# Spreading a chunk's score, value, state and output groups differently over its four steps

## What is computed

```python
# attention layer: 16 heads of size 64 for Q and K, 16 for V, 12 levels
Q, K, V = x @ Wq.T, x @ Wk.T, x @ Wv.T
dt  = softplus(x @ Wdt.T + dt_bias);  cg = cumsum(-exp(A_log) * dt, axis=1)
Lam = softplus(Lp * (x @ Wdl.T))
W[t,s] = (Q[t] . K[s]) / 8 * exp(cg[t] - cg[s]) * Lam[t, level(t, s)]   # s <= t
o = (W @ V) @ Wout.T + x;  x = layernorm(x + layernorm(o) * ln_g + ln_b)
# recurrent layer over the 2 entries, 256 features
c = sigmoid(x wf + c uf + bf) * c + sigmoid(x wi + c ui + bi) * tanh(x wc + c uc + bc)
x = layernorm(x + tanh(x wo + c_final uo + bo))
```

## Time and profile before

| | us |
|---|---|
| three runs | 703.26, 699.67, 698.87 |
| median | 699.67 |
| the profiled execution's own time | 703.26 |
| its span, first to last instruction | 701.5 |

### The profile page before, as it was taken

How to read it: one execution, slowest core, us unless ns; L and a number is a source line. 1 busy time by engine, 2 the same in 40 slices (tenths; PEclk the granted TensorE clock), 3 DMA queues, 4 the chain that set the end, 5 groups by cost and what they waited for, 6 DMA issues and landing times.

```text
span 701.5 us, 22072 instructions
## 1 busy us (share of the span) xinstructions
PE 670.3 (96%) x9172; PEld 603.3 (86%) x9172; DVE 475.2 (68%) x1067; ACT 339.6 (48%) x759; POOL 355.5 (51%) x476
## 2 busy tenths in 40 slices
PE   5889999999999999999999999999997999999994
PEld 3779999998999999899999999999986788888894
DVE  2843768688776968675877769686877445454546
ACT  4545455544444453555444444545443434555555
POOL 1652755645564646466565636565464224344434
PEclk9989999999999999999999999999999899999997
DMA  8020312203050402112150503121222000000002
GB/s 296 26 57 18 80 40 58 68 31 96 3 95 7 92 21 78 35 33 64 35 95 3 95 9 90 35 63 49 35 66 93 1 1 0 31 32 31 30 31 91
DMA packets 53588, 37.09 MB, mean 53 GB/s; under 512 B 5360, under 2 KB 52080, under 8 KB 53488
## 3 DMA queue, kind: packets, MB, share of 16 engines
q1 hardware_dynamic: 53488, 35.67, 20.2%
HBM read 30.41 MB, written 5.24 MB: 51 GB/s over the span
## 4 chain that ended last, share of the span: by engine, by line
PE 88%; DVE 3%; DMA 2%; POOL 2%; ACT 2%; SPq 1%; issue 1%; DVEq 0%; ACTq 0%
PE bank L378 64%; PE bank L381 6%; PE bank L467 5%; PE bank L400 5%; PE bank L432 4%; PE bank L496 4%; SPq L325 1%; DMA xt<-in_wffn 1%; DMA bv<-in_bcv 1%; DVE t L966 1%; ACT t L735 1%; POOL wL L1333 1%; POOL t L1333 0%; DVE ng L963 0%; DVE t L963 0%
## 5 line engine op out<-in xcount | busy, mean ns | idle before, releaser
L378 PE MATMUL bank<-xH,wH 128*128 128x256 f32 x480 | 148.3, 309 | 2.4 <-ACT KT L735 1.1
L378 PE MATMUL bank<-xL,wH 128*128 128x256 f32 x480 | 136.1, 284 | 0.0
L378 PE MATMUL bank<-xH,wL 128*128 128x256 f32 x480 | 135.5, 282 | 0.0
L735 ACT ACTIVATE QT<-bank 128x512 f32<-128x512 f32 x64 | 38.2, 597 | 144.1 <-PE bank L378 144.1
L963 DVE TENSOR_TENSOR W<-bank,E 128x512 f32<-128x512 f32 x128 | 82.2, 684 | 35.6 <-PE bank L378 35.6
L378 PEld LDWEIGHTS bank<-xH,wH 128*128 128x128 f32 x480 | 91.4, 190 | 10.2 <-issue 9.0
L378 PEld LDWEIGHTS bank<-xL,wH 128*128 128x128 f32 x480 | 91.7, 191 | 0.4
L378 PEld LDWEIGHTS bank<-xH,wL 128*128 128x128 f32 x480 | 91.7, 191 | 0.0
L735 ACT ACTIVATE E<-bank 128x512 f32<-128x512 f32 x128 | 66.1, 603 | 17.4 <-PE bank L400 17.4
L378 PE MATMUL bank<-QT,KT 64*128 64x128 f32 x1024 | 65.9, 279 | 0.6 <-ACT E L735 0.6
L735 ACT ACTIVATE KT<-bank 128x512 f32<-128x512 f32 x64 | 38.0, 594 | 54.1 <-PE bank L378 54.0
(11 more groups left out here) (149 smaller groups left out, 1660.5 us busy)
## 6 DMA issues: line engine op xcount, KB each, us to landing
cB<-scr SPq DMA_DIRECT2D x240, 64.0 KB, 3.0
xt<-in_xT SPq DMA_DIRECT2D x16, 256.0 KB, 3.7
xs<-in_x SPq DMA_DIRECT2D x16, 256.0 KB, 4.1
out<-xs SPq DMA_DIRECT2D x16, 256.0 KB, 2.1
xt<-in_wffn SPq DMA_DIRECT2D x8, 256.0 KB, 3.2
QT<-in_wqk SPq DMA_DIRECT2D x4, 256.0 KB, 5.8
KT<-in_wqk SPq DMA_DIRECT2D x4, 256.0 KB, 6.9
scr<-cT SPq DMA_DIRECT2D x16, 64.0 KB, 1.9
```

The costliest lines, as they stand in the source:

```text
L378: return e.matmul(o, a, b, start=start, stop=stop)
L735: return e.activation(o, i, f, **kw)
```

## The change

It touches no instruction's operands, only the order on PE, ACT and DVE, and with it the order in which the two shared banks are handed out (`misc_jobs`). On PE, weigh(ci-1, 1) goes from n = 0 to n = 1, behind inter; scores(ci, 1) goes from n = 1 to n = 2; state goes from n = 3 to n = 2, behind scores(ci, 1); out_proj(ci-1) goes from n = 2 to n = 3; turn_coefs goes in front of the projection of its step. ACT takes turn_coefs in front of the projection's copy. DVE takes turn_y and out_proj one step later and state one step earlier.

```diff
--- before.py
+++ after.py
@@ -76,7 +76,7 @@
             out += [("keys", ci, 0), ("keys", ci, 1)]
         if s % 4 == 1 and cc:
             out += [("inter", ci, 0), ("inter", ci, 1)]
-        if s % 4 == 3 and cc < CB - 1:
+        if s % 4 == 2 and cc < CB - 1:
             out += [("state", ci, 0)]
     for sg, j in token_jobs(s):
         if j == 3:
@@ -690,27 +690,28 @@
                     exponents(ci)
                 if (c1 := chunk_at(s, 4)) is not None:
                     weigh(c1, 0)
-                    weigh(c1, 1)
                 if 0 <= ci < NC:
                     if n == 0:
                         keys(ci)
                     if n == 1:
                         scores(ci, 0)
-                        scores(ci, 1)
                         if ci in INTER:
                             inter(ci)
-                    if n == 3 and ci in STATE:
-                        state(ci)
-                if (c1 := chunk_at(s, 6)) is not None:
+                    if n == 2:
+                        scores(ci, 1)
+                        if ci in STATE:
+                            state(ci)
+                if (c1 := chunk_at(s, 5)) is not None:
+                    weigh(c1, 1)
+                if (c1 := chunk_at(s, 7)) is not None:
                     out_proj(c1)
                 for sg, j in token_jobs(s):
                     if j == 3:
                         decays(sg)
+                    if j == 5:
+                        turn_coefs(sg)
                 for sg, j in project_jobs(s):
                     project(sg, j)
-                for sg, j in token_jobs(s):
-                    if j == 5:
-                        turn_coefs(sg)
                 for sg, j in token_jobs(s):
                     if j == 0:
                         tokens(sg)
@@ -929,11 +930,11 @@
                     act(c0H[:, :, :], bc(c0, 2, 2), ACT.Copy).then_inc(a_c0, 1)
                 if 0 <= s < NG and s % 4 == 0:
                     keys(s // 4)
-                for sg, j in project_jobs(s):
-                    project(sg, j)
                 for sg, j in token_jobs(s):
                     if j == 5:
                         turn_coefs(sg)
+                for sg, j in project_jobs(s):
+                    project(sg, j)
                 for sg, j in token_jobs(s):
                     tokens(sg, j)
                 if 0 <= s - NG + 9 < 8:
@@ -1284,14 +1285,14 @@
             turn_levels(0)
             split_wq(2, 1)
             for s in STEPS:
-                if (ci := chunk_at(s, 5)) is not None:
+                if (ci := chunk_at(s, 6)) is not None:
                     turn_y(ci)
                 if 0 <= s < NG and s % 4 in (1, 2):
                     weights(s // 4, s % 4 - 1)
                 for sg, j in token_jobs(s - 1):
                     if j in (5, 7):
                         turn_levels(2 * sg + (j - 5) // 2)
-                if (ci := chunk_at(s, 6)) is not None:
+                if (ci := chunk_at(s, 7)) is not None:
                     out_proj(ci)
                 if s == FIRST_FFN:
                     first_bias()
@@ -1313,7 +1314,7 @@
                             last_norm()
                 if 0 <= s < NG and s % 4 == 1 and s // 4 in INTER:
                     inter(s // 4)
-                if 0 <= s < NG and s % 4 == 3 and s // 4 in STATE:
+                if 0 <= s < NG and s % 4 == 2 and s // 4 in STATE:
                     state(s // 4)
                 for sg, j in token_jobs(s):
                     tokens(sg, j)
```

## The result

| | before | after |
|---|---|---|
| median of four runs, us | 699.27 (698.41 to 703.26) | 721.63 (718.55 to 724.53) |
| the profiled execution's own time | 703.26 | 721.02 |
| its span | 701.5 | 719.2 |

The ratio is 1.031 with an interval of 1.026 to 1.036: slower. The median is 7.1 us more than the 714.5 that was forecast and 0.6 us above the upper end of the range of 706 to 721. Profiled execution against profiled execution the change costs 17.8 us, where +10.7 had been worked out; median against median it costs 22.4 us.

The account below looks back on a forecast made before the run. PE was taken to set the pace in the 28 chunks with projections. Terms 9.5 + 3.8 + 4.5 - 4.7 - 2.4 = +10.7 gave 714.0 from 703.26, or 714.8 from 699.67; forecast 714.5 us, range 706 to 721.

Parts of the forecast that it names:

- Switches of shape: On PE, cutting weigh and scores in halves pays entry and exit twice: 0.34 us a chunk, +9.5 us (0 to +14).
- The projections' one bank: With out_proj alone between two projections, PE waits 0.26 us for ACT's copy, +7.0 us; with savings +3.8 together.
- The stall of state: In every second chunk, the projection behind state loses a 0.17 us stall from ACT's late copy: -2.2 us.
- chunk 15: Without state, a projection waits 1.14 us behind another; out_proj now fits in, about -1.0 us.
- turn_coefs in front: turn_coefs waits about 0.3 us per supergroup for DVE to read inter's k = 0 bank: +4.5 us (0 to +7).
- The other engines: In the steady part, later or earlier work on DVE and SP costs nothing, covered by DVE's idle quarter.
- DVE becomes late in n = 2: Rival: exponents or keys wait for DVE's row behind scores(ci, 1), 0.5 us a chunk, 728 us; chance 0.09.
- The first chunk: scores(0, 1) and state(0) fill PE's idle time before decays; clock stays full, exponents(1) near 50.4: -4.7 us.
- Behind the last projection: turn_coefs(15) comes 2.0 us earlier and the chain to the recurrent layer moves with it: -2.4 us (-3.5 to +1).

Follow-up runs that it names:

- b2: Kernel before, with only scores(ci, 1) moved behind inter within n = 1: 708.23 us, ratio 1.010.
- a4: Changed kernel with turn_coefs back behind the projection (PE, ACT) and weigh undivided in n = 0 on PE: 713.05 us, ratio 1.016.
- d1: Changed kernel with out_proj put behind the projection of n = 3, nothing between the projections of n = 2 and n = 3: one execution, 742.12 us.
- a1: Changed kernel with turn_coefs put back behind the projection on PE and ACT: 717.66 us, ratio 1.021.
- c1: Changed kernel with DVE alone taking state one step later (n = 3, behind out_proj), PE as changed: 720.85 us, ratio 1.028.
- a3: Changed kernel with both halves of scores in n = 1 again, in front of inter: 720.64 us, ratio 1.027.
- b1: Kernel before, with only turn_coefs put in front of the projection on PE and ACT: one execution, 710.44 us.
- e0: Kernel before with state(0) at n = 2 and out_proj of even chunks in n = 3 ahead of state: 701.49 us, ratio 0.999.
- c2: Changed kernel with its last chunks in the order of before, turn_coefs staying in front: 716.90 us, ratio 1.024.
- a2b: Changed kernel with state back at n = 3 on PE and DVE, a single execution for its trace: 431.81 us from chunk 2 to 28.

## Why the prediction was right or wrong

**Switches of shape: right, in mechanism and size.** Forecast 0.15 for weigh and 0.19 for scores. In chunk 4 weigh's halves take 1.15 for 1.01 (+0.14) and those of scores 2.18 for 1.99 (+0.19). b2 and a4 price them alone at 0.20 and 0.135 us. The rule that the prediction cited from the Trainium skill, TensorEngine Tiling (Array Packing), Tiling Modes, Key Properties, that a change of tiling mode drains the array, agrees with b2: there the work and the banks stay, only the shapes alternate once more. The step from inter to weigh and that from scores to state were not free, which had been open.

**The projections' one bank: the wait is there, its price was mis-sized.** The floor of 1.06 us holds in the trace after, and d1 shows that it is the bank. The step that failed is the price: the term 1.06 - 0.80 = 0.26 us took out_proj's 0.68 from the earlier trace rows, and in the same rows the projection behind it takes 1.69 us to state (67.40 to 69.09), where a projection elsewhere takes 1.5 to 1.6: the distance of 0.68 was short only because the projection's record starts while out_proj still streams, and the rest was in the next distance. In chunk 5 out_proj goes from 0.67 to 0.94, and the four projections together from 6.40 to 6.20: 0.07 us net, not 0.27. In the even chunk the price is 0.14 (out_proj +0.08, decays +0.10, projections -0.04), part of it the step from state to decays that the forecast had let cancel. At 26 chunks this term came out at 2.7 us (13 x 0.14 + 13 x 0.07) instead of 6.8. The stall of state went as forecast (1.21 to 1.04), and chunk 15 changed by -0.37 us, where the forecast's terms give 0.34 + 0.30 - 1.0 = -0.36.

**turn_coefs in front: right.** 0.29 us in chunk 5 against 0.3, longer where inter is short (chunks 1 and 17, where putting it back gains more). a1 puts it at 2.5 us for the 26 chunks; the forecast has 3.9, since it left out that tokens and the projections get shorter by 0.1 us when turn_coefs moves to the front.

**The other engines: wrong, this is the missed term.** The step "I cost this at nothing; the cover is DVE's idle quarter" failed. It looked at weights, CT and state, and not at bank YB, which weigh shares with out_proj. DVE is idle for 20 of the 80 us, but at the wrong place: in chunks 8 and 24 PE waits 1.3 us for oo (+1.34 beyond the ordinary 0.50 each, +2.7 together), and chunks 12 and 28 pay 0.2. c1 shows the mechanism, a3 shows how little room there was. The rival "DVE becomes late in n = 2" had the engine right, but another bank, and would have charged every chunk. Since 2.9 us were missed here and 4.1 charged too much at the bank, the sum of the 26 chunks looked right: 16.3 forecast, 15.5 measured.

**The first chunk: half right.** The idle time was filled as forecast (3.05 to 1.12 us in front of decays). The stretches after, columns as in the earlier trace rows, and PE's timeline:
```profile
45.00:50.00 5.00, 3.88 (x21) 3.61 (x20) 4.97 (x10) 1.03 (x2) 0.96 (x1) 0.68 0.00 0
50.00:55.00 5.00, 4.22 (x68) 3.56 (x68) 3.44 (x6) 2.65 (x5) 1.40 (x1) 0.97 0.00 2
```
```profile
43.94 1.11 PE L496 MATMUL bank<-Vw,Kt 128*64 128x16 f32 x32
46.17 0.63 PE L378 MATMUL bank<-ng,cs 128*128 128x32 f32 x4 [1.12 <-DVE ng L964]
46.64 1.02 PE L378 MATMUL bank<-cs,ng 128*128 128x128 f32 x4
```
The clock fell to 1.2 GHz all the same, for 3.4 us instead of 10.2. Exponents of chunk 1 start at 52.83, not 50.4. The step that failed is the one that tied the clock to the 3.05 us of idle time. b1 and b2 have before's order there and idle as long in front of decays (3.05 and 3.06 us), yet their clock is low for 3.4 us only; from X(0) to X(1) they take 17.56 and 17.27 us, after and a1 17.05 and 16.92, and the profiled execution of before, with its long stretch at the low clock, 19.64. So most of the -2.2 us is the length of that stretch in one execution of before, and 0.2 to 0.5 us is what the change brings. The prediction also took it that the two faster executions of before probably had no clock drop there; they have no trace, but the clock fell at this place in all thirteen traces read here, in e0's too, an execution of 701.83 us.

**Behind the last projection: wrong in sign.** Forecast -2.4, measured +3.2. turn_coefs(15) came 2.0 us earlier in its chunk, but the load of recurrent weights only 1.0 us, and E of chunk 31 was then held by its exponents and these by CT. So nothing was gained at the start of the chain; and behind E it got longer, from the start of scores(31) to the gates' first transposes (L381, cs and xs): 9.40 us before (535.41 to 544.81), 13.84 after:
```profile
545.62 2.09 PE L400 MATMUL bank<-CT,AT 32*128 32x128 f32 x32 [2.04 <-DVE CT L1189]
...
547.78 2.06 ACT L736 ACTIVATE E<-bank 128x512 f32<-128x512 f32 x4 [0.19 <-PE bank L400]
...
549.68 1.16 PE L378 MATMUL bank<-QT,KT 64*128 64x128 f32 x16
...
551.05 2.00 PE L467 MATMUL bank<-QT,S 64*32 64x128 f32 x127 [0.21 <-ACT Kt L736]
...
554.42 0.27 PE L467 MATMUL bank<-QT,S 64*32 64x128 f32 x1 [1.36 <-issue]
...
554.62 0.64 PE L432 MATMUL bank<-W,V 128*32 128x128 f32 x16
...
555.19 1.16 PE L378 MATMUL bank<-QT,KT 64*128 64x128 f32 x16
...
561.68 2.05 PE L378 MATMUL bank<-wo,yt 128*128 128x256 f32 x4
...
563.52 1.91 PE L381 MATMUL bank<-cs,xs 128*128 128x128 f32 x8
```
A half of weigh (0.57), a stall of 1.36 us inside inter, and a second entry of scores now lie in that chain, where the old order had them in front of it or not at all. With 0.3 for the entry they are 2.5 of the 4.4 us more. The other 1.9 are the clock: it falls at 558.8 us, in the midst of the 36 products of two columns for the gates, and not at 544.0, at their end, so these take 5.40 us instead of 4.53 and out_proj 1.85 instead of 0.78. Against the 4.4 us stand 1.3: scores(31, 0) starts 4.06 us behind exponents(31) (549.68 to 545.62) instead of 5.38, since the other half of weigh and the wait for E no longer precede it. The rest nearly cancels: X(31) comes 1.1 us later behind X(29) (27.3 instead of 26.2), and from the transposes to the end it is 1.0 us less. The last part runs at the low clock (from 560 to 565 us):
```profile
560.00:565.00 5.00, 5.00 (x20) 4.53 (x21) 1.08 (x4) 0.38 (x1) 1.22 (x2) 0.50 0.00 0
```
c2 puts the old order back there and has 197.2 us for the tail. The prediction had named the danger in half a sentence ("weigh(31, 1) now cuts into the gate groups") and priced it at nothing beyond the bound of +1.

**The sum.** Against 714.0, the profiled 721.02 is 7.0 us more: the tail 5.6 (+3.2 for -2.4), everything up to X(2) 2.1 (-1.7 for -3.8), less 0.7 from X(2) to X(29) (16.2 for 16.9). The forecast of 714.5 against the median before, 699.67 then, was +14.8; the medians moved by 22.4. That the total came so near the range is in part luck: 2.9 us of waits on DVE that were at nothing and 4.1 us too much for the bank offset each other.

## What to carry to other kernels

Where one engine sets the pace, an order that alternates more often between array shapes costs its switches in every round (here 0.14 us for weigh and 0.20 for scores), whatever it does for latency: count the entries and exits of each shape, not the instructions. Read the price of a group together with that of its successor, since a short distance can be borrowed from the next one; and when a group is moved, list every reader of every bank that it or its neighbours write, on each engine's list, and look for the rounds in which such a reader has extra work. The loop's last rounds are a chain of latencies: what is a free delay in the steady part is paid there in full, and it can be left in the old order.

## What had not been expected of the hardware

- The clock fell to 1.2 GHz behind 1.12 us of idle time in the trace after, and behind 3.05 us before; how long it stayed low does not follow that idle time: 3.4 us in most profiled executions (behind 1.12 us of it after, 2.01 in e0, 3.05 in b1, 3.06 in b2), 10.2 us in two (behind 2.16 in a2b, 3.05 before). In the tail it was low for 17.1 us in one stretch (from about 553 to 570 us) in a1 and c1, whose tails take 207.0 and 205.5 us against 200.9.
- In the tail after, PE was recorded as busy for 5.00 of 5.00 us at a granted clock of 0.50 (the row above), within and behind a row of 36 products of 2 columns each (556.28 to 561.46).
- In the kernel after, DVE's two adds of S over 192 columns took 2.32 us together while POOL was adding tiles of 416 columns; they took 1.19 us in c1, where POOL's adds ended at 169.71, halfway through:
```profile
169.14 1.19 DVE L964 TENSOR_TENSOR S<-S 128x192 f32<-128x192 f32 x2
```
- The stall of 1.36 us inside inter of chunk 31, between its 127th and its last record, is put down to no other engine. It stands at the same record in a1 (1.96 us), a2b (0.57), c1 (1.58) and d1 (1.40), that is in every kernel that has both scores and weigh in halves there, and in none that leaves one of them whole (a3, a4, b2, c2 and before among them); no run explains it.
